# Graph attention edge steps: weights multiplied into the gathered rows instead of into the one-hot matrices

## The reference

```
e     = leaky_relu(el[src] + er[dst])           # per edge and head
ex    = exp(e - segment_max(e, dst)[dst])
denom = segment_sum(ex, dst)
out   = segment_sum(z[src] * ex / denom[dst], dst) + x + b ; elu
```

## Time and profile before

| what | value |
|---|---|
| median of 3 runs | 4994.68 us (4993.73 to 4998.18) |
| the profiled execution | 4996.26 us, span 4994.3 us |
| PE, PEld busy | 3297.9 us (66%), 2364.7 us (47%) |
| DVE, ACT, POOL busy | 2336.7 us (47%), 1328.5 us (27%), 2463.1 us (49%) |
| mean granted TensorE clock | 0.602; about 0.5 in the two attention layers |
| software DMA queue (the gathers) | 119808 packets, 334.13 MB, 24.2% of 16 engines |

### The profile page before, as it was taken

One profiled execution on the slowest core, in us unless ns is written; L12 is line 12 of the kernel. 1 busy time (PEld: TensorE's weight loads), 2 busy tenths in 40 slices (PEclk: granted clock), 3 DMA queues, 4 the chain that ended last, 5 costly groups with the idle time before them and its releaser, 6 DMA issues. The chain is left out here.

```text
span 4994.3 us, 105041 instructions
## 1 busy us (share of the span) xinstructions
PE 3297.9 (66%) x33900; PEld 2364.7 (47%) x33901; DVE 2336.7 (47%) x7260; ACT 1328.5 (27%) x4738; POOL 2463.1 (49%) x2519
## 2 busy tenths in 40 slices
PE   4576677667677774666666666665566666666665
PEld 3344444444444443555555555554455555555554
DVE  6445444445444443444444444443444444444444
ACT  5221121221121221333333333332222222222222
POOL 2444444444444443555555555552555555555552
PEclk9677777777777766555555555555555555555555
DMA  7322222222222222333333333332333333333332
GB/s 231 108 81 80 79 78 81 81 81 77 80 77 81 82 79 74 88 90 93 92 96 90 90 94 92 95 90 60 91 94 96 92 92 92 98 91 91 91 98 62
DMA packets 259185, 450.20 MB, mean 90 GB/s; under 512 B 83953, under 2 KB 162357, under 8 KB 259007
## 3 DMA queue, kind: packets, MB, share of 16 engines
q0 software_dynamic: 119808, 334.13, 24.2%
q1 hardware_dynamic: 139327, 115.47, 7.6%
HBM read 389.29 MB, written 60.10 MB: 90 GB/s over the span
## 5 line engine op out<-in xcount | busy, mean ns | idle before, releaser
L1460 POOL DMA_INDIRECT nodes<-z_rows,scratch x1664 | 1599.0, 961 | 1432.6 <-PE ge_part L1542 540.4
L961 POOL DMA_INDIRECT scratch<-h_rows,scratch x832 | 832.4, 1000 | 992.6 <-DVE nodes L1099 700.1
L1712 DVE TENSOR_TENSOR scratch<-scratch,ge_runs 128x32 f32<-128x32 f32 x208 | 43.6, 209 | 1193.2 <-PE ge_runs L1516 1187.1
L1005 PE MATMUL ce_part<-nodes,scratch 128*32 128x128 f32 (+1 forms) x6656 | 443.8, 404 | 178.7 <-DVE nodes L1099 118.7
L1537 PE MATMUL ge_part<-nodes,scratch 128*32 128x64 f32 x13312 | 449.9, 314 | 162.1 <-DVE scratch L1720 85.3
L1430 ACT COPY scratch<-ge_part 128x260 f32<-128x260 f32 x208 | 78.0, 375 | 1706.0 <-remote 1607.9
L1537 PEld LDWEIGHTS ge_part<-nodes,scratch 128*32 128x32 f32 x13312 | 350.8, 168 | 206.0 <-issue 139.3
L1005 PEld LDWEIGHTS ce_part<-nodes,scratch 128*32 128x32 f32 x6656 | 256.9, 144 | 368.2 <-issue 198.6
L1551 PE MATMUL ge_sum<-scratch 128*128 128x128 f32 x832 | 245.1, 447 | 256.3 <-ACT scratch L1430 256.3
L985 PE MATMUL ce_w<-fc_sb,scratch 64*128 64x256 f32 x1664 | 317.6, 513 | 102.2 <-ACT scratch L892 100.1
L1099 DVE TENSOR_TENSOR nodes<-ce_w,scratch 128x768 f32<-128x768 f32 x416 | 376.4, 945 | 0.0
(11 more groups left out here) (217 smaller groups left out, 5945.4 us busy)
## 6 DMA issues: line engine op xcount, KB each, us to landing
nodes<-z_rows,scratch POOLq DMA_INDIRECT x1664
nodes<-hT SPq DMA_DIRECT2D x56, 256.0 KB
scratch<-x SPq DMA_DIRECT2D x52, 256.0 KB, 3.8
scratch<-h_rows,scratch POOLq DMA_INDIRECT x832
z_rows<-scratch SPq DMA_DIRECT2D x28, 264.0 KB
z_rows<-nodes SPq DMA_DIRECT2D x28, 264.0 KB
nodes<-x_skip SPq DMA_DIRECT2D x28, 256.0 KB
x_rows<-nodes SPq DMA_DIRECT2D x28, 256.0 KB
```

The costliest lines, as they stand in the source:

```text
L961: nc.gpsimd.indirect_dma_start(xg[u][:, i * D:(i + 1) * D], None, m.h_rows, bass.IndirectOffsetOnAxis(ap=idx[r][:, k:k + 1], axis=0)).then ...
L1005: ins = nc.tensor.matmul(here, hots[u][:, at:at + TW], these, start=(q == 0 and c == 0), stop=(q == 1), skip_group_check=True)
L1460: nc.gpsimd.indirect_dma_start(zg[r][:, k * ZW:(k + 1) * ZW], None, m.z_rows[layer], bass.IndirectOffsetOnAxis(ap=idx[r][:, k:k + 1], axis ...
```

## The change

`hots` and the 32-column weighting go. In their place stands `zs`: 8 tiles of 260 columns, of which 256 are `z[src] * ex` by head and 4 are `ex` itself, written there by exp. VectorE scales the even tiles (two instructions of 128x512), ScalarE the odd ones (16 instructions of 64 columns with `ex` as the scale). `tile_sums` becomes one matmul per tile: plain one-hot times the 260 columns. POOL's gathers wait for the scaling engines (`zs_ready`, `zs_act_ready`) instead of for TensorE; `half_summed` is gone. Since `ex` and `zs` have one buffer, exp of a step waits until the tile sums of the step before are done.

```diff
-        hots = scratch(G * HEADS * TW)
+        zs = scratch(G * (D + HEADS))
-        ex = [scratch(LANES) for u in range(2)]
+        by_tile = zs.rearrange("p (k w) -> p k w", k=G)
+        ex = by_tile[:, :, D:D + HEADS]
...
+                act.wait_ge(part_summed, v + 1)
                 act.wait_ge(diff_ready, v + 1)
-                nc.scalar.activation(ex[u], diff[u], ACT.Exp).then_inc(ex_ready, 1)
+                nc.scalar.activation(ex, lanes(diff[u]), ACT.Exp).then_inc(ex_ready, 1)
...
-                act.wait_ge(part_summed, v + 4)
                 act.wait_ge(ex_ready, v * 2 + 2)
-                for k in range(G // 2 + 1, G, 2):
+                for k in range(1, G, 2):
                     for h in range(HEADS):
-                        ins = nc.scalar.activation(weighted(k, h), one_hot(r, k), ACT.Copy,
-                                                   scale=ex[u][:, h * (G + 1) + k:h * (G + 1) + k + 1])
-                ins.then_inc(hots_act_ready, 1)
-                act.wait_ge(part_summed, v + 5)
+                        ins = nc.scalar.activation(by_tile[:, k, h * HF:(h + 1) * HF],
+                                                   zg[r][:, k * ZW + h * HF:k * ZW + (h + 1) * HF], ACT.Copy,
+                                                   scale=by_tile[:, k, D + h:D + h + 1])
+                ins.then_inc(zs_act_ready, 1)
+                act.wait_ge(part_summed, v + 2)
...
-                for q, released in ((0, half_summed), (1, part_summed)):
-                    pool.wait_ge(released, v + 1).then_inc(pool_go, 1)
+                for q in range(2):
+                    pool.wait_ge(zs_ready, v * 2 + 2).then_inc(pool_go, 1)
+                    if q == 1:
+                        pool.wait_ge(zs_act_ready, v + 1).then_inc(pool_go, 1)
...
-                pe.wait_ge(hots_ready, v * 2 + (q + 1))
                 if q == 0:
+                    pe.wait_ge(zs_ready, v * 2 + 10)
                     pe.wait_ge(sums_ready, v + 1)
                 else:
-                    pe.wait_ge(hots_act_ready, v + 1)
-                for h in range(HEADS):
-                    for j in range(NB):
-                        k = 2 * j + q
-                        ins = nc.tensor.matmul(ps_part[j * TW:(j + 1) * TW, h * HF:(h + 1) * HF], weighted(k, h),
-                                               zg[r][:, k * ZW + h * HF:k * ZW + (h + 1) * HF],
-                                               start=(q == 0 and h == 0), stop=(q == 1), skip_group_check=True)
+                    pe.wait_ge(zs_act_ready, v + 5)
                 for j in range(NB):
                     k = 2 * j + q
-                    ins = nc.tensor.matmul(ps_part[j * TW:(j + 1) * TW, D:D + HEADS], one_hot(r, k),
-                                           lanes(ex[r % 2])[:, k, :], start=False, stop=(q == 1), skip_group_check=True)
+                    ins = nc.tensor.matmul(ps_part[j * TW:(j + 1) * TW, 0:D + HEADS], one_hot(r, k), by_tile[:, k, :],
+                                           start=(q == 0), stop=(q == 1), skip_group_check=True)
...
+            def weighted_rows(r, tiles):
+                z = zg[r].rearrange("p (k w) -> p k w", k=G)[:, tiles, 0:D].rearrange("p k (h f) -> p k h f", h=HEADS)
+                out = by_tile[:, tiles, 0:D].rearrange("p k (h f) -> p k h f", h=HEADS)
+                weight = ex[:, tiles].rearrange("p k (h o) -> p k h o", o=1)
+                count = len(range(tiles.start, tiles.stop, tiles.step))
+                return V.tensor_tensor(out, z, weight.broadcast_to([P, count, HEADS, HF]), ALU.mult)
...
-                dve.wait_ge(part_summed, v + 4)
-                weighted_one_hots(r, 0)
+                dve.wait_ge(part_summed, v + 1)
+                weighted_rows(r, slice(0, 3, 2)).then_inc(zs_ready, 1)
                 if ahead >= 1:
                     over_tiles(v + 1, 1 - u)
-                weighted_one_hots(r, 1).then_inc(hots_ready, 1)
+                weighted_rows(r, slice(4, 7, 2)).then_inc(zs_ready, 1)
                 add_window(v - 1, 1 - u, base)
-                weighted_one_hots(r, 0, 1).then_inc(hots_ready, 1)
```

More of the change, by code:

```diff
@@ L1289, in gat_stage @@
          er_ready, raw_ready, score_ready, eT_ready, ends_ready, lv_ready, state_ready, ini_ready, init_ready, fwd_ready,
-         max_ready, maxT_ready, diff_ready, ex_ready, hots_ready, hots_act_ready, half_summed, part_summed, sums_ready, scaled,
+         max_ready, maxT_ready, diff_ready, ex_ready, zs_ready, zs_act_ready, part_summed, sums_ready, scaled,
          summed, added) = [
@@ L1294, in gat_stage @@
                              "eT_ready", "ends_ready", "lv_ready", "state_ready", "ini_ready", "init_ready", "fwd_ready",
-                             "max_ready", "maxT_ready", "diff_ready", "ex_ready", "hots_ready", "hots_act_ready",
-                             "half_summed", "part_summed", "sums_ready", "scaled", "summed", "added")]
+                             "max_ready", "maxT_ready", "diff_ready", "ex_ready", "zs_ready", "zs_act_ready",
+                             "part_summed", "sums_ready", "scaled", "summed", "added")]
         block = ctx.enter_context(nc.Block())
@@ L1306, in one_hot @@
             return hot[r][:, at:at + TW]
-        def weighted(k, h):
-            at = (k * HEADS + h) * TW
-            return hots[:, at:at + TW]
+        by_tile = zs.rearrange("p (k w) -> p k w", k=G)
+        ex = by_tile[:, :, D:D + HEADS]
         @block.sync
@@ L1462, in step @@
                             bass.IndirectOffsetOnAxis(ap=idx[r][:, k:k + 1], axis=0)).then_inc(got[r], 16)
-            pool.sem_inc(half_summed, 4)
             all_steps(pool, last_quad, step)
@@ L1582, in _ @@
             pe.sem_inc(sums_ready, 1)
-            pe.sem_inc(part_summed, 4)
+            pe.sem_inc(part_summed, 1)
             pe.sem_inc(hotT_ready, 1)
@@ L1603, in step @@
                     line_up(v + 1)
-                tile_sums(v, r, 0).then_inc(half_summed, 1)
+                tile_sums(v, r, 0)
                 if ahead >= 1:
@@ L1712, in differences @@
                 V.tensor_tensor(lanes(diff[u]), lanes(score[u]), lanes(ps_max), ALU.subtract).then_inc(diff_ready, 1)
-            def weighted_one_hots(r, half, q=0):
-                tiles = slice(half * NB // 2, (half + 1) * NB // 2)
-                out = hots.rearrange("p (a q h n) -> p a q h n", q=2, h=HEADS, n=TW)[:, tiles, q]
-                one = hot[r].rearrange("p (q a o n) -> p a q o n", q=2, o=1, n=TW)[:, tiles, q]
-                by = ex[r % 2].rearrange("p (h e o) -> p e h o", h=HEADS, o=1)[:, q:G:2][:, tiles]
-                return V.tensor_tensor(out, one.broadcast_to([P, NB // 2, HEADS, TW]),
-                                       by.broadcast_to([P, NB // 2, HEADS, TW]), ALU.mult)
+            def weighted_rows(r, tiles):
[4 more added lines that the diff above has]
+                return V.tensor_tensor(out, z, weight.broadcast_to([P, count, HEADS, HF]), ALU.mult)
             def scale_first(v, u, base):
@@ L1775, in _ @@
             V.memset(node.zero, 0.0)
+            dve.sem_inc(zs_ready, 8)
+            dve.sem_inc(zs_act_ready, 4)
             dve.sem_inc(s_pR, 1)
```

## The result

The changed kernel takes 5254.76 us (median of 4 runs, 5250.8 to 5272.67), the kernel before 4996.43 us (4993.73 to 4999.45): ratio 1.0524, 95% interval 1.0499 to 1.0549. It is slower by 5.2%, where 3.8% faster was forecast. The profiled execution took 5250.8 us, span 5248.7.

The account below looks back on a forecast made before the run. No engine was full; the tile sums' end, seen late while POOL gathers, was taken as the wait that starts everything else. 4996 - 256 + 75 - 15 = 4800, stated as 4805 us, range 4640 to 5120.

Parts of the forecast that it names:

- Part 1: Tile sums' end, seen 3.80 us late beside gathers: fewer matmuls make it prompt, window sums stop waiting, gain 256 us.
- part 5: POOL's gathers: released earlier, eight run without a pause for 10.0 us of a 13 us step; no gain, no cost.
- Part 2: VectorE's weighting: three 128x256 instructions become two 128x512 ones at 673 ns, costing 75 us in total.
- Part 3: ScalarE's weighting: sixteen 64-column instructions take 4.0 us, hidden ahead of the odd tile sums; cost nothing.
- Part 4: TensorE's tile sums: wide matmuls overlap, a half takes 1.05 us instead of 1.15; gain 15 us in all.
- Rival A: Tile sums' signal stays held until POOL pauses, whatever the number of matmuls: about 5790 us; chance 0.12 with its like.
- Rival B: Tile-sum records drip out singly beside gathers, one per 0.7 us, so part 1's gain is gone: about 5055 us; chance 0.18.

Follow-up runs that it names:

- the first comparisons: The first three rounds of follow-up runs, each with the kernel before run alongside: it took 5083.84, 5073.98 and 5074.21 us.
- e17: The kernel before, unaltered, run again for its trace: 4050.27 us.
- e7: The changed kernel, with POOL waiting between its two groups of gathers until the first group's rows have landed: ratio 0.9727.
- e11: The changed kernel with a 128x720 memset on POOL, and a wait for it, ahead of both groups of gathers: ratio 0.9537.
- e16: The same program as e11, run again beside a kernel before of about 4050 us: ratio 1.0427.
- the first trace: The profiles belonging to the result: the changed kernel at 5250.8 us, the kernel before at 4996.26 us.
- e15: The changed kernel, unaltered, run again beside a kernel before of about 4050 us: ratio 1.0132.
- e9: The changed kernel with a 128x1440 memset on POOL, and a wait for it, between the two groups of gathers: ratio 0.9812.
- e18: The changed kernel with VectorE's second scaling cut from two tiles to one, tile 6 left unscaled: ratio 1.0024.
- e1: The changed kernel with each 260-column tile-sum matmul cut into four pieces, 48 more matmul records a step: ratio 1.2007.
- e5: The changed kernel with only the even tile sums cut into four pieces a tile, 24 more matmul records a step: ratio 1.1411.
- e12: The changed kernel with a 128x120 memset on POOL, and a wait for it, ahead of both groups of gathers: ratio 1.0145.
- e14: The kernel before with a 128x720 memset on POOL and its wait in the middle of each group of four gathers: ratio 1.0427.
- e13: The changed kernel with both tile sums cut into four pieces a tile and a 128x720 memset ahead of both groups of gathers: ratio 1.1146.

## Why the prediction was wrong

**Part 1, the late end: the step that failed.** "If the number of instructions is what makes the end late, it comes 0.07 us after the last matmul" held for that batch (0.06 us). What failed is what stood behind it: "Behind them TensorE itself is the bound", the term of -256 us, and with it part 5's "no cost while POOL has 3 us to spare", a term put at nothing. The wait for the copy did go, and the loops still took 245 us more. I treated the late end as a property of one batch. It is one of the stream: while the condition of the first comparisons holds, what TensorE ends late in eight unpaused gathers is seen late in most steps. In the kernel before the thing regulated itself: the late end of the odd sums held back POOL's second group, and that pause of some 1.8 us, with one of 2 us or more ahead of the next first group, let TensorE catch up twice a step. (Without late ends the same kernel makes no such pause: in e17 eight gathers and more follow one another.) With short tile sums the signal comes in time, the second group follows without a pause, and the maxima at the end of the burst are late instead, where nothing covers them. e7 puts the pause back and changes nothing else: 1.052 becomes 0.973. e11 puts both back: its loops run as fast as where no end is late (e16).

What it cost: the loops give (15.35 - 12.82 + 15.14 - 12.28) x 99 = 534 us between the first trace and e15, and (14.05 - 12.58 + 13.96 - 12.03) x 99 = 337 us between the earlier trace rows and e17. So the condition with late ends costs the changed kernel 197 us more than the kernel before. With the 54.5 us of its own work that is 252 of the measured 258 us. This is a split of the loss and no second proof of it, since 197 is itself the difference of the two kernels' differences; that it is the late ends is what e7, e9, e11 and e16 show.

**Part 2, VectorE: right in the main.** Two scalings of 664 ns (673 assumed). Here is the way to the even sums in the changed kernel:

```profile
2786.58 0.67 DVE L1713 TENSOR_TENSOR scratch<-nodes,scratch 128x512 f32<-128x512 f32 x1
2787.44 0.66 DVE L1713 TENSOR_TENSOR scratch<-nodes,scratch 128x512 f32<-128x512 f32 x1
2788.14 0.20 PEld L1535 LDWEIGHTS ge_part<-scratch 128*32 128x32 f32 x8 [1.26 <-DVE scratch L1713]
```

The sum without its first term was 75 - 15 = +60 us; without late ends the change costs 54.5, and e18 shows that most of it is VectorE's.

**Part 3, ScalarE: right.** Sixteen scalings last 3.93 us (4.0); the odd sums wait 2.0 us for them in the whole run. **Part 4: right in kind.** The four wide matmuls overlap: 1.10 us a half (1.05), so a half gained 0.05 us where 0.1 was taken. **Part 5**: most gathers at a pitch of 1.25 us, as said, and VectorE waits only 15.5 us for rows in the whole run; the price was not in POOL's time but in TensorE's ends.

**Rival A** had the mechanism (a signal held until POOL pauses, worse because POOL no longer pauses) with the wrong place: it held the tile sums in every step and gave 5790 us. They were mostly in time; what came after them was not, by 1 to 4 us in most steps. I gave it 0.12, since short batches were seen at once beside gathers. That end lay 1.6 us behind the start of its group of gathers; I didn't ask how long since the last pause each prompt end was. **Rival B** gave 5055 us by a slow leak, which e1 shows at work; here it takes hold later. The time, 5255 us, lies between B and A, above the range (4640 to 5120).

**What stays open.** What the backlog is, and why it is there in three comparisons (before: 5074 to 5084 us, and 4996 in the first trace) and absent in three (4049 to 4052 us); the stages ahead of attention are faster there too (differences first start at 1976 us in the first trace, at 1414 in e17). There ScalarE's copy L924, behind the convolution's L1005, idles 607.6 us for "remote" in the first trace and not at all in e17, so the late ends are not peculiar to attention. The Trainium skill ("NOTIFIC — the notification-queue block", section 7.1, on overflow) says that the block which writes trace records holds up its producers when its own queues fill. That would fit what e1 and e5 show, that each instruction of TensorE counts; no run here shows that it is the cause. Every run on record has a span and a clock that the profiler read, so none tells whether the late ends are there at all when nothing is recorded. The shortest pause that clears the late ends (e12) and the cure in the kernel before (e14) stay open too, as their comparison had none.

## What to carry to other kernels

Where an end is seen late, ask what clears the lateness, and whether the change takes that away: a wait that looks like the loss can be the pause that keeps the rest in time. Look at every signal of that engine against the time since the last pause, not at the one that is late now. And run the kernel before again beside every version, the changed one too, which I didn't do in the first three comparisons: a gain that hangs on such a condition (e11: 0.954 and, as e16, 1.043) is not one of the kernel.

## What the runs showed of the hardware

- The same kernel took 4996 to 5084 us and 4049 to 4052 us, with the gather at 0.95 us and the granted clock of the attention stages at 0.50 to 0.54 in both. In the convolution the granted clock was lower with late ends: 0.73 (300 to 1900 us of the first trace) against 0.84 (200 to 1350 us of e17).
- With late ends, TensorE's ends were mostly seen 0.8 to 1.9 us after the last gather of a burst, in some steps while it still ran; 1.5 us without a gather every four let nearly all through (e11: no difference late, 39 of 208 copies late, half of them by 1 us or less), POOL being busy with a memset meanwhile.
- 48 more matmul records a step with the same columns cost 3.8 us with late ends and no pauses (e1), and 1.46 us without late ends ((1.1146 - 1.0427) x 4050 / 200, e13 and e16, both with pauses).
- Beside VectorE's scaling a gather lasted 1.74 us instead of 0.95 (e15 above); of some 195 gathers of e15 beside a scaling, 77 took over 1.3 us. POOL had the time for it: VectorE waited 23.9 us for gathered rows in the whole run. The Trainium skill ("SBUF — State Buffer", on the shared port pair) says that a VectorE instruction with two SBUF inputs and a GpSimd instruction that reads SBUF lock each other out. The trace agrees in direction; no run isolates such a lock from the rest of VectorE's work in that stretch.
